# Attention results divided by the softmax sums inside the attention stage instead of in the last stage

## What is computed

```python
x = x + attn(layernorm(x))
x = x + ffn(layernorm(x))

# attn: layer norm again, q, k, v = projections, rotary tables on q and k
sim  = einsum('bhid,bhjd->bhij', q, einsum('bhnd,hde->bhne', k, W_bilinear))
attn = softmax(sim, axis=-1)                  # exp(sim - max) / sum
out  = einsum('bhij,bhjd->bhid', attn, v)     # heads side by side
return out @ Wo

# ffn: ternary weights w1, w2
h = layer_norm(x, ln1_g, ln1_b) @ w1.T + b1
h = gelu(h)
return layer_norm(h, ln2_g, ln2_b) @ w2.T + b2
```

## Time and profile before

| | |
|---|---|
| median of 3 runs | 3641.97 us (3637.11 to 3646.02) |
| profiled execution | 3640.75 us, its span 3639.0 us |
| busy in the span | PE 3455.4, POOL 2807.4, DVE 2559.4, ACT 2312.8 us |
| mean granted clock of TensorE | 0.985 |
| the chain that ended last | x_in transfers 5%, down_bank 2%, y_bank 2%, zn_lo 1%, turn_c 1%, x_gained 1% |

### The profile page before, as it was taken

How to read it: one execution, slowest core, us unless ns; L and a number is a source line. 1 busy time by engine, 2 the same in 40 slices (tenths; PEclk the granted TensorE clock), 3 DMA queues, 4 the chain that set the end, 5 groups by cost and what they waited for, 6 DMA issues and landing times. The chain is left out here.

```text
span 3639.0 us, 71328 instructions
## 1 busy us (share of the span) xinstructions
PE 3455.4 (95%) x21150; PEld 2234.0 (61%) x21150; DVE 2559.4 (70%) x4312; ACT 2312.8 (64%) x4404; POOL 2807.4 (77%) x1343
## 2 busy tenths in 40 slices
PE   6999999999999999999999999999999967888888
PEld 4655555555555555555555555666666637777777
DVE  6666666666666666666666666666666657897797
ACT  2766666666666666666666666676666744444444
POOL 2888888888888888888888888888888944554453
PEclk8999999999999999999999999999999989999999
DMA  5223222322232222222322222222221325555553
GB/s 193 82 86 106 86 86 86 105 87 87 87 103 87 85 87 103 87 87 87 105 87 89 86 101 88 87 86 104 77 77 59 106 62 126 140 133 131 130 134 90
DMA packets 304944, 356.31 MB, mean 98 GB/s; under 512 B 40544, under 2 KB 229472, under 8 KB 300128
## 3 DMA queue, kind: packets, MB, share of 16 engines
q1 hardware_dynamic: 295392, 343.89, 30.6%
q10 hardware_dynamic: 9216, 8.39, 0.7%
HBM read 220.08 MB, written 62.13 MB: 78 GB/s over the span
## 5 line engine op out<-in xcount | busy, mean ns | idle before, releaser
L446 POOL TENSOR_TENSOR prob_sum<-prob_sum,prob 128x1024 f32<-128x1024 f32 x762 | 1876.5, 2463 | 292.7 <-ACT prob L525 242.0
L676 DVE TENSOR_REDUCE row_max<-max_scores 128x1 f32<-128x512 f32 x1536 | 986.9, 683 | 610.0 <-PE max_scores L790 595.5
L525 ACT ACTIVATE prob<-scores 128x512 f32<-128x512 f32 x2048 | 1073.1, 600 | 374.2 <-PE scores L744 363.5
L923 PE MATMUL attn_out<-prob,v 128*64 128x512 f32 x4096 | 935.4, 598 | 0.0
L735 PE MATMUL scores<-q_hi,k_hi 64*128 64x512 f32 x2048 | 776.5, 416 | 12.4 <-ACT scores L496 8.2
L744 PE MATMUL scores<-q_lo,k_hi 64*128 64x512 f32 x2048 | 749.9, 394 | 0.0
L740 PE MATMUL scores<-q_hi,k_lo 64*128 64x512 f32 x2048 | 747.2, 393 | 0.0
L923 PEld LDWEIGHTS attn_out<-prob,v 128*64 128x64 f32 x4096 | 271.2, 136 | 547.6 <-issue 545.3
L790 PE MATMUL max_scores<-k_hi,q_hi 64*128 64x512 f32 x1536 | 575.4, 427 | 6.7 <-DVE rows L666 2.8
L496 ACT ACTIVATE scores<-neg_max_seeds 128x512 f32<-128x512 f32 x1024 | 553.2, 603 | 13.2 <-DMA neg_max_seeds<-neg_max_halves 13.2
L735 PEld LDWEIGHTS scores<-q_hi,k_hi 64*128 64x128 f32 x2048 | 375.9, 184 | 286.0 <-issue 159.1
(11 more groups left out here) (138 smaller groups left out, 5022.1 us busy)
## 6 DMA issues: line engine op xcount, KB each, us to landing
rows<-rows SPq DMA_DIRECT2D x512, 128.0 KB, 2.0
neg_max_seeds<-neg_max_halves SPq DMA_DIRECT2D x128, 512.0 KB, 4.0
w_group<-w_parts SPq DMA_DIRECT2D x30, 1536.0 KB, 6.8
attn_normalised<-z_stage SPq DMA_DIRECT2D x128, 256.0 KB, 2.1
v<-attn_normalised SPq DMA_DIRECT2D x64, 512.0 KB, 9.6
z_inverse<-sums_inverted SPq DMA_DIRECT2D x128, 256.0 KB, 10.3
x_turned_parts<-x_tile_parts SPq DMA_DIRECT2D x49, 256.0 KB, 4.2
xt_batch<-x_turned_parts SPq DMA_DIRECT2D x7, 1792.0 KB, 10.5
```

The lines of the kernel that those rows point to most:

```text
L446: nc.gpsimd.tensor_tensor(sums_of(k, half), a, prob[:, n % RING, :, :], ALU.add).then_inc(added, 1)
L525: nc.scalar.activation(prob[:, n % RING, e, :], S[e][n % 2][:, :], ACT.Exp).then_inc(exped[e], 1)
L676: nc.vector.reduce_max(mx[1 - u][:, e, n // 2, n % 2:n % 2 + 1], bank_of(e, jj)[:, :], axis=AX.X)\
L923: nc.tensor.matmul(O[rows(e), :], V[k // 2 % 2][:, j, col:col + DH], prob[:, n % RING, e, :], start=j == 0, stop=j == 7).then_inc(pv_made[ ...
```

## The change

The inverse of each pair is written to one small DRAM buffer and read back at once, spread over the partitions (`load_inverse`, two transfers of 256 KB in pieces of 2 KB, into the new tile `inv_rows`). VectorE multiplies the staged results of pair t - 2 by it in quarter 0 of span t (`norm_z`), and only then does SyncE store them; `z_stage` gets a second pair of buffers for that. The last pair's sums are made over all 64 rows of each head by TensorE (`sums_last`) and inverted and applied by VectorE without a transfer (`norm_last`). The last stage loads no inverses, has no GpSimd product and no lag NORM. `pairs` writes out four spans ahead of the loop instead of three.

```diff
-            for t in (-2, -1, 0):
+            for t in range(-2, FIRST):
...
+            def load_inverse(t):
+                wait(sp, inv_out, 16 * (t + 1))
+                at_rest()
+                wait(sp, z_made, 2 * t)
+                at_rest()
+                for e in two:
+                    sp.dma_start(inv_rows[rows(e), :, :], inv_scr[:, e, :].partition_broadcast(DH)).then_inc(inv_in, 16)
...
-                if k >= 1:
-                    store_z(t - 1, 1)
+                if k >= 2:
+                    for h in two:
+                        store_z(k - 2, t - 2, h)
...
                 if k >= 1:
                     store_inverse(t - 1)
-                if attn:
-                    store_z(t, 0)
                 if prep:
                     max_seeds(t, 1)
+                if k >= 1:
+                    load_inverse(t - 1)
...
-                wait(act, z_stored[h], 16 * t)
-                nc.scalar.activation(zst[h][:, :], O[:, :], ACT.Copy).then_inc(z_copied, 1)
+                wait(act, z_stored[h], 16 * (t - 1))
+                nc.scalar.activation(zst[k % 2][h][:, :], O[:, :], ACT.Copy).then_inc(z_copied, 1)
...
+            def norm_z(k, t):
+                wait(dve, inv_in, 32 * (t + 1))
+                for h in two:
+                    wait(dve, z_copied, 2 * t + h + 1)
+                    z = zst[k % 2][h]
+                    nc.vector.tensor_tensor(z[:, :], z[:, :], inv_rows[:, h, :], ALU.mult).then_inc(z_made, 1)
+
+            def norm_last(h):
+                for e in two:
+                    wait(dve, seeded[e], 8 * (T - 1) + 4)
+                wait(dve, l_made, 4 * (T - 1) + 2 * h + 2)
+                nc.vector.reciprocal(seeds[:, 0, h, :], (M, X[0])[h][:, :]).then_inc(last_inv, 1)
+                dve.wait_ge(last_inv, h + 1)
...
+                nc.vector.tensor_tensor(z[:, :], src[:, :], seeds[:, 0, h, :], ALU.mult).then_inc(z_made, 1)
...
                         if proj:
                             rotate(t, Q)
+                    if q == 0 and k >= 2:
+                        norm_z(k - 2, t - 2)
...
-            invert(T - 1)
+            norm_z(T - 2, T - 2)
+            norm_last(0)
+            norm_last(1)
...
+            def sums_last(h):
+                if h:
+                    pe.wait_ge(added_last, 7)
...
+                for e in two:
+                    nc.tensor.matmul((M, X[0])[h][rows(e), :], ones[:, :], sums_of(T - 1, h)[:, e, :], start=True, stop=True)\
+                        .then_inc(l_made, 1)
...
-        LOAD, NORM, SPLIT, Y_MADE, UP, GATE, DOWN, RES = range(8)
+        LOAD, SPLIT, Y_MADE, UP, GATE, DOWN, RES = range(7)
...
-                    wait(sp, z_normed, t - 1)
-                    sp.sem_inc(sp_carrier, 1)
-                    for e in two:
-                        sp.dma_start(zi[r % 2][e * DH:(e + 1) * DH, :, :],
...
-                if at(j, q, NORM):
-                    t, r = at(j, q, NORM)
-                    pool.wait_ge(z_in[r % 2], 16 * (t >> 1) + FREE)
-                    pool.wait_ge(inv_in[r % 2], 32 * (t >> 1) + 32)
-                    nc.gpsimd.tensor_tensor(za[r % 2], za[r % 2], zi[r % 2][:, :, :], ALU.mult).then_inc(z_normed, 1)
...
-                    wait(act, z_normed, t + 1)
+                    act.wait_ge(z_in[r % 2], 16 * (t >> 1) + FREE)
```

More of the change, by code:

```diff
@@ L157 @@
 BODY = 3 * PAIRS
+FIRST = 2
 RING = 8
@@ L202, in attention @@
         ones_full = sb("ones_full", [P, P], F)
-        zst = [sb(f"z_stage{h}", [P, HALF], F) for h in two]
+        zst = [[sb(f"z_stage{u}{h}", [P, HALF], F) for h in two] for u in two]
+        inv_rows = sb("sum_inverted_rows", [P, 2, HALF], F)
         sum_rows = sb("sum_rows", [P, HALF], F)
@@ L275, in _ @@
         def _(sp):
-            for s in swap_in[K] + swap_in[Q] + z_stored + nm_in + nm_out + seed_in + [x_in, l_in, inv_out] + x_stored:
+            for s in swap_in[K] + swap_in[Q] + z_stored + nm_in + nm_out + seed_in + [x_in, l_in, inv_out, inv_in] + x_stored:
                 sp.sem_inc(s, CREDIT)
@@ L411, in _ @@
             pairs(sp, span)
-            store_z(T - 1, 1)
-            sum_columns(T - 1)
-            store_inverse(T - 1)
+            for t in (T - 2, T - 1):
+                for h in two:
+                    store_z(t, t, h)
             for h in two:
                 wait(sp, z_stored[h], 16 * T)
-            wait(sp, inv_out, 16 * T)
             for u in two:
@@ L589, in invert @@
                 nc.vector.reciprocal(inv[:, :], sum_cols[:, :]).then_inc(inv_made, 1)
+            def norm_z(k, t):
+                wait(dve, inv_in, 32 * (t + 1))
+                for h in two:
+                    wait(dve, z_copied, 2 * t + h + 1)
[7 more added lines that the diff above has]
+                dve.wait_ge(last_inv, h + 1)
+                z = zst[(T - 1) % 2][h]
+                if h == 0:
+                    wait(dve, z_copied, 2 * (T - 1) + 1)
+                    src = z
+                else:
+                    for e in two:
+                        wait(dve, pv_made[e], 16 * T)
+                    wait(dve, z_stored[1], 16 * (T - 2))
+                    src = O
+                nc.vector.tensor_tensor(z[:, :], src[:, :], seeds[:, 0, h, :], ALU.mult).then_inc(z_made, 1)
             def statistics(t, u):
@@ L795, in turn_max, with sums @@
                 nc.tensor.transpose(X[1][:, 0:P], negm[:, :], ident[:, :]).then_inc(nm_turned, 1)
-            def sums(k, t, last=False):
-                if last:
-                    wait(pe, added, 14 * t + 7)
-                    pe.wait_ge(added_last, 7)
-                else:
-                    wait(pe, added, 14 * t + 14)
+            def sums(k, t):
+                wait(pe, added, 14 * t + 14)
                 for h in two:
@@ L807, in sums @@
                             .then_inc(l_made, 1)
+            def sums_last(h):
+                if h:
+                    pe.wait_ge(added_last, 7)
+                    pe.wait_ge(ffn_scaled, 3)
+                else:
+                    wait(pe, l_copied, T - 1)
+                    wait(pe, added, 14 * (T - 1) + 7)
+                for e in two:
+                    nc.tensor.matmul((M, X[0])[h][rows(e), :], ones[:, :], sums_of(T - 1, h)[:, e, :], start=True, stop=True)\
+                        .then_inc(l_made, 1)
             def span(k, t, b):
@@ L911, in span @@
                             sums(k - 1, t - 1)
+                        if k == T - 1 and q == 3:
+                            sums_last(0)
                         half = q // 2
@@ L925, in _, with feed_forward @@
             pairs(pe, span)
-            wait(pe, l_copied, T - 1)
-            sums(T - 1, T - 1, True)
-def feed_forward(nc, x, z_scr, inv_scr, kept, alpha, g1, b1, g2, b2, bias2, ident_in, out):
+            sums_last(1)
+def feed_forward(nc, x, z_scr, kept, alpha, g1, b1, g2, b2, bias2, ident_in, out):
     RT = ROWS // P
@@ L947, in feed_forward @@
         halfpow = sb("halfpow3", [P, 1], F)
-        zi = [sb(f"z_inverse{u}", [P, PAIRS, P], F) for u in two]
         zhi = [sb(f"zn_hi{u}", [P, PAIRS, P], R) for u in two]
@@ L977, in feed_forward @@
         shift_made, folded = sem("shifts_made3"), sem("shifts_folded3")
-        z_in, x_in, inv_in = ([sem(f"{n}3_in{u}") for u in two] for n in ("z", "x", "inv"))
-        z_normed = sem("p3_z_normed")
+        z_in, x_in = ([sem(f"{n}3_in{u}") for u in two] for n in "zx")
         (z_hi, z_lo, y_made, x2_made, stats_b, aggr_b, var_b, up_scaled, xg_made, b_turned, ht_hi, ht_lo, up_made,
@@ L1049, in _ @@
         def _(pool):
-            for s in (z_normed, up_scaled, down_scaled, x2b_made):
+            for s in (up_scaled, down_scaled, x2b_made):
                 pool.sem_inc(s, FREE)
```

41 lines of the change are left out of this document (19 added, 22 removed).

## The result

The changed kernel takes 3537.77 us (median of 4 runs, 3532.18 to 3537.86), against 3641.4 us for the kernel before on the same chip: a ratio of 0.9711, 95% interval 0.9695 to 0.9728. The forecast was 3530 us. Its profiled execution took 3532.18 us, with a span of 3530.2 us and a mean granted clock of 0.991.

A forecast was written before the change was run, and what follows sets the result against it. TensorE paces the attention; in the last stage, with no engine full, product stalls and late transfers set the step. 3640.75 - 108 (steps) - 4 (start) = 3528.7 us profiled, plus 1.2 gives 3530; range 3512 to 3548 us (0.68).

The forecast's parts named there:

- The step of the last stage: Last stage, one x_after_attn to the next: falls from 9.82 to 8.1 us, 108 us gained over 63 steps.
- The loop between TensorE and VectorE: Last stage: TensorE 5.94 us, VectorE 1.81 us and 0.2 us behind up_bank, together 7.95 us a step.
- two full engines that lose a little to each other: Last stage: TensorE and VectorE about equally full, so 8.1 us a step was taken instead of 7.95.
- Two causes: Last stage's 9.82 us step: VectorE stands still beside GpSimd's product, and x_in queues behind z_lo, results and spread inverses.
- the granted clock in a rival: Last stage stays partly late through clock below 1.00 or late x_in: 8.5 to 9.2 us a step, 3555 to 3600; chance 0.15.
- The rival that the loads stay the bound at 9.4 us a step: Last stage: nothing but GpSimd's product goes, 9.4 us a step, 3612 us; chance 0.05.
- The attention at 0: Attention's 60 spans: norm_z's two products, 1.2 us alone, fit VectorE's 3.90 us idle time before quarter 1's first maximum.
- the worst case of the earlier trace: Attention, quarter 0: norm_z waits 1.8 us for GpSimd's additions and ends 0.6 us ahead of need.
- the rival of inverses that land too late: Attention: inverses land 1 to 2 us after 1045, TensorE waits up to 1 us a span, 3545 to 3590; chance 0.06.
- The price without the cover: Attention, norm_z without VectorE's idle time: 60 x 1.2 = 72 us, with GpSimd's lock up to 60 x 3.0 = 180 us.
- my "slower" rival: Attention: both norm_z products meet whole GpSimd additions, 6.0 us, 2.1 beyond cover, 126 us in 60 spans, 3656 us; chance 0.04.
- The end of the attention: After VectorE's last additions: norm_z products, two 3.0 us inversions, two more products; last stage begins at 2974.0, 4.4 us later.

The follow-up runs named there:

- the one with the new order: The changed kernel with the wait for y_bank moved last, behind those for x_in and x2b_made, ahead of x_after_attn: 3528.48 us, ratio 0.9693.

## Why the prediction was right, and where it was off

**The step of the last stage.** Predicted 8.1 us, measured 8.12; 63 steps gave 618.9 - 511.4 = 107.5 us of the 108 forecast. The loop between TensorE and VectorE holds as well: the written-out steps run at its 7.95 us. My reason for the 0.15 us above it, two full engines that lose a little to each other, is wrong. VectorE was busy 91.4 us in 100, 7.4 us a step, near the lower end of what I had given it, and with its zn_lo out of the way the step stayed. The term that was too small is the last of 5.94 + 1.81 + 0.2: I took the 0.2 us between up_bank and x_after_attn from the last step, which is written out, and in the loop it is 0.42, because the wait for y_bank stands two instructions ahead. That makes 8.17, and 8.16 was measured in the loop. The allowance of 0.15 us for another reason came near the missing 0.22 by luck. (The upper bound of 8.8 us was called half of the way back; that would be 8.96. Nothing hangs on it.)

**Two causes.** The prediction named both and priced only their removal together; the runs show why nothing less would do (13 and 22 us singly, 113 together). It had the granted clock in a rival only; in fact the clock's return from 0.95 to 1.00 is some 0.4 us of the 1.7 a step. The rival that the loads stay the bound at 9.4 us a step falls with them, but what the prediction held against it, that x_in gets a step more, is not the reason: without that step x_in lands in 3.8 us as soon as the inverses' 512 KB are gone.

**The attention at 0.** Right: 45.07 and 45.06 us a span with and without the products. As predicted for the worst case of the earlier trace rows, norm_z waited for the rest of GpSimd's addition, and the rival of inverses that land too late did not come up. That the port pair is locked for a whole instruction (the Trainium skill, "SBUF — State Buffer", SBUF: two separate sides) agrees with 3.05 us in place of 1.2 here, and with 5.24 us where both products met a GpSimd instruction.

**The price without the cover.** Here I was wrong: 72 to 180 us were said, and 382 us measured. The 3.0 us a span stood for one wait of a product for GpSimd; both waited, as in my "slower" rival (6.0 us), and a stall of 4.46 us at TensorE cost another 1.7 us behind it, at half the clock, which no sentence had. That rival's own size must be corrected in the same way: its 2.1 us beyond the cover would have been the least that it costs.

**The end of the attention.** Two large inversions took 3.35 us each, not 3.0: 0.7 us. The slope from 16 to 512 columns is 6.3 ns a column, between the 5.5 ns from the rows and the 8.4 ns (4.3 us over 512 columns) of my estimate from the Trainium skill's page "VectorE: DVE Perf Modes" (First, the fixed hardware budget). VectorE's additions also ended 2.1 us later than before (2964.59 against 2962.48): the span in which the loop of spans begins anew took 49.5 us instead of 46.6. TensorE was idle in it for 2.2 us of "issue" where it had been 0.8, and behind the longer of the two pieces (1.84 us) its granted clock was 0.51 from 1264.5 to 1268.0 us, which costs 1.7 us more. Why the "issue" is longer stays open; in the other profiles of the changed kernel, with norm_z in its place, that span took 49.7 to 53.1 us. Together the stage began 2.7 us later than forecast (2976.7 against 2974.0), and its first x_after_attn came 22.5 us behind instead of 22.0: 3.3 us in all.

**The sum.** Forecast for a profiled execution 3528.7 us. Adding 3.3 us for the start and 1.0 us for the steps (511.4 instead of 63 x 8.1 = 510.3) gives 3533.0; it took 3532.18. To the median I added 1.2 us; it lies 5.6 us above the profiled execution here, and that is 4.4 of the 7.8 us from 3530 to 3537.77. The granted clock was 0.991 in the profiled execution and 0.988 to 0.989 in the other three.

## What to carry to other kernels

Where two waits end within the same step, price the removal of each alone and of both: either of them can be worth almost nothing by itself and the pair a hundred microseconds. Put a VectorE instruction with two SBUF inputs where GpSimd runs out of work and where VectorE would wait anyway; elsewhere each of the two here waited for a GpSimd instruction, and behind TensorE's stall came a stretch at half its clock as well. For the wait that is met last, look in the trace which instruction carries it: one or two waiting instructions between it and the work cost 0.1 and 0.22 us a step here. Look again after the edit, since the order in the source does not decide it alone.

## What the runs showed of the hardware

A stall of TensorE cost more than its length. After it had been busy 1.54 us in 6, TensorE was granted 0.50 of its clock for about 3.5 us (a product of 512 columns took 0.62 us instead of 0.39), which made a stall of 4.46 us cost 6.2.

Two VectorE instructions in a row do not share one wait for GpSimd: in the kernel with norm_z at the end of quarter 1, GpSimd began its next instruction between them, and the two took 5.24 us; where GpSimd had only the rest of one addition left they took 3.05, alone they would take 1.2.

The same transfer landed much later under a heavier load. The 128 KB of x_in took 3.7 to 3.8 us to land in the kernels whose last stage moved 80 to 95 GB/s, and 9.2 to 10.6 us in those that moved 133 to 134. The size of what stands ahead in the queue and the rate changed together here, so the runs do not part the two.

From y_bank's release to x_after_attn it took 0.02 us where x_after_attn carried the wait, 0.12 us where the wait was on the instruction directly ahead, and 0.23 to 0.25 us where a second waiting instruction stood between the two. In the changed kernel the short way is that of the steps written out, in the one with the new order that of one step in eight of the loop, while the steps written out have 0.12: it goes with the place of the wait and not with the loop.
